# A twelve-stage perceiver: each layer norm is prepared in quarters inside the loop of the layer before

## The reference

```
def _layernorm(x, axis=-1, eps=1e-05):
    m = jnp.mean(x, axis=axis, keepdims=True)
    v = jnp.var(x, axis=axis, keepdims=True)
    return (x - m) / jnp.sqrt(v + eps)
...
x = x + _L0_xattn_ref(_layernorm(x), ctx_1024, ctx_1024, mask_BxSxS2_bk1, ...)
x = x + _L0_attn_ref(_layernorm(x), ...)
x = x + _L0_ffn_ref(_layernorm(x), ...)
...                       # L1: xattn, attn, ffn;  L2: xattn, attn, ffn;  L3: xattn, attn
x = x + _L3_ffn_ref(_layernorm(x), ...)
```

## Time and profile before

| | |
|---|---|
| median of 3 runs | 3710.66 us (3710.53 to 3714.74) |
| the profiled execution, its own time | 3704.09 us |
| its span, first to last instruction | 3702.4 us |
| mean granted TensorE clock | 0.913 of full speed |
| busy in the span | PE 3084.8 (83%), DVE 2010.6 (54%), ACT 1339.0 (36%), POOL 694.3 (19%) |

### The profile page before, as it was taken

The page is one execution under the profiler, slowest core; times in us unless marked ns, Lnnn a source line. Parts: engine busy times, 40 slices in busy tenths (PEclk is TensorE's granted clock), DMA queues, the critical chain, the costliest instruction groups (busy, mean ns, idle before and its releaser), DMA issues. The chain is left out here.

```text
span 3702.4 us, 64870 instructions
## 1 busy us (share of the span) xinstructions
PE 3084.8 (83%) x23914; PEld 1980.6 (53%) x23914; DVE 2010.6 (54%) x6137; ACT 1339.0 (36%) x3783; POOL 694.3 (19%) x1501
## 2 busy tenths in 40 slices
PE   6999987777779977887678885555999999999799
PEld 5888875555447755555446663333444444444465
DVE  4888875556236666669865556654232322332544
ACT  1444432333238762244367774432111111111222
POOL 1333330000027740033115652100000000000000
PEclk8999998988889998878689997777999999999899
DMA  3000000000011110210031100005000000000100
GB/s 90 25 24 25 26 21 1 1 1 1 4 34 43 42 36 3 56 43 1 16 62 38 34 25 15 1 1 176 1 1 1 1 1 1 1 1 1 39 1 12
DMA packets 164817, 83.61 MB, mean 23 GB/s; under 512 B 78803, under 2 KB 158678, under 8 KB 164310
## 3 DMA queue, kind: packets, MB, share of 16 engines
q1 hardware_dynamic: 164502, 79.47, 8.4%
HBM read 75.75 MB, written 3.67 MB: 21 GB/s over the span
## 5 line engine op out<-in xcount | busy, mean ns | idle before, releaser
L3074 PE MATMUL bank<-WhhT,hT 128*64 128x512 f32 (+1 forms) x4096 | 681.4, 488 | 29.6 <-ACT hT L3137 29.6
L3074 PEld LDWEIGHTS bank<-WhhT,hT 128*64 128x64 f32 x4096 | 285.7, 137 | 374.1 <-issue 256.4
L1188 POOL TENSOR_SCALAR probs<-probs,rinv 128x257 f32<-128x257 f32 x512 | 236.8, 482 | 169.8 <-DVE rinv L1099 169.7
L1005 ACT ACTIVATE probs<-probs,nbias 128x257 f32<-128x257 f32 x512 | 254.7, 507 | 0.0
L3226 DVE TENSOR_TENSOR pr<-hb,bank 128x512 f32<-128x512 f32 x32 | 22.0, 688 | 343.4 <-PE bank L3116 343.4
L3251 POOL COPY rb<-hT 128x512 f32<-128x512 f32 x32 | 35.7, 1117 | 919.8 <-ACT hT L3137 898.5
L925 PE MATMUL bank<-ident,probs 128*128 128x128 f32 x1024 | 141.0, 281 | 63.2 <-POOLq L1189 63.1
L729 POOL TENSOR_SCALAR probs<-probs,rinv 128x257 f32<-128x257 f32 x256 | 120.1, 482 | 277.0 <-DVE rinv L667 277.0
L925 PEld LDWEIGHTS bank<-ident,probs 128*128 128x128 f32 x1024 | 110.4, 141 | 93.6 <-POOLq L1189 84.9
L551 ACT ACTIVATE probs<-bank,nbias 128x257 f32<-128x257 f32 x256 | 119.3, 472 | 81.8 <-DVE rinv L667 71.1
L477 PE MATMUL bank<-kvT,qh 128*128 128x257 f32 x512 | 136.7, 391 | 4.5 <-ACT kvT L542 4.5
(11 more groups left out here) (658 smaller groups left out, 6874.9 us busy)
## 6 DMA issues: line engine op xcount, KB each, us to landing
kvT<-in_ctx_T SPq DMA_DIRECT2D x128, 128.5 KB
raw<-in_L_ffn_gru_w_hh SPq DMA_DIRECT2D x24, 512.0 KB, 4.7
kv<-in_ctx SPq DMA_DIRECT2D x64, 128.0 KB
kv<-in_ctx SPq DMA_DIRECT2D x32, 256.0 KB
W<-in_L_ffn_W SPq DMA_DIRECT2D x64, 64.0 KB, 2.2
v_last<-v_last SPq DMA_DIRECT2D x192, 8.0 KB, 1.7
mask_u<-in_mask_BxSxS_bk SPq DMA_DIRECT2D x64, 32.1 KB, 1.9
mask_u<-in_mask_Bx1xSxS_bf SPq DMA_DIRECT2D x64, 32.1 KB, 2.0
```

What stands on the lines that cost most here:

```text
L1005: i = e.activation(s, s, ACT.Exp, bias=self.nbias[v][:, r:r + 1], scale=self.scale, accum_out=self.rows_sum[v][:, r:r + 1])
L1188: e.tensor_scalar(s, s, self.rinv[v][:, r:r + 1], 1.0, ALU.mult, ALU.mult)
L3074: mm = e.matmul(self.bank[b][hf * BATCH:(hf + 1) * BATCH, 0:n], lhs, rhs, start=start, stop=stop, tile_position=(0, hf * BATCH))
```

## The change

X is loaded by four transfers, one for each quarter. Quarters 0, 1 and 2 of the next layer's norm are made in the loop of the layer before: VectorE takes the statistics once the last tile of the quarter has its update (`next_statistics`), and POOL makes the reciprocal root by Newton steps and the rows of y (`next_rows`). VectorE does all of quarter 3 after it has closed the stage. A tally `normed` takes the place of `norm_row`. ScalarE's Sqrt is removed from the norm; the stages that have a second norm of their own keep theirs. The last layer's norm runs over X in its normal order, and ScalarE puts yT in the order of time when it copies it; SP stores X behind the last quarter, and the reload is awaited only by the experts.

```diff
-    def norm_dve(self, e):
...
-    def norm_act_std(self, e):
...
+    def norm_statistics(self, e, layer, q):
+
+        tiles = range(4 * q, 4 * q + 4)
+        self.normed.wait_ge(e, 4 * (layer - 1) + q + 1)
+        for t in tiles:
+            e.bn_stats(self.stats[:, 6 * t:6 * t + 6], self.X[:, t * P:(t + 1) * P])
+        e.drain()
+        for t in tiles:
+            e.bn_aggr(self.moments[:, 2 * t:2 * t + 2], self.stats[:, 6 * t:6 * t + 6])
+        if q < 3:
+            e.drain().then_inc(self.measured.up(), 1)
+        else:
+            e.drain()
+            h, r, z = self.first_root(e, q)
+            for _ in range(3):
+                e.tensor_tensor(z, r, r, ALU.mult)
+                e.drain()
+                e.tensor_tensor(z, z, h, ALU.mult)
+                e.drain()
+                e.scalar_tensor_tensor(r, z, 1.5, r, ALU.add, ALU.mult)
+                e.drain()
+            self.norm_rows(e, q)
+            self.normed.wait_ge(e, 4 * layer + 3)
+            e.drain().then_inc(self.normed.up(), 1)
+
+    def norm_pool(self, e, layer, q):
+
+        self.measured.wait_ge(e, 3 * layer + q + 1)
+        h, r, z = self.first_root(e, q)
+        for _ in range(3):
+            e.tensor_tensor(z, r, r, ALU.mult)
+            e.drain()
+            e.tensor_tensor(z, z, h, ALU.mult)
+            e.drain()
+            e.tensor_scalar(z, z, 1.5, None, ALU.add)
+            e.drain()
+            e.tensor_tensor(r, r, z, ALU.mult)
+            e.drain()
+        self.norm_rows(e, q)
+        e.drain().then_inc(self.normed.up(), 1)
+
+    def first_root(self, e, q):
...
+        e.tensor_scalar(h, var, 1e-5, -0.5, ALU.add, ALU.mult)
+        e.drain()
+        e.tensor_scalar(r.bitcast(I32), h.bitcast(I32), -0.5, float(0x5f3759df - (1 << 30) - (1 << 22)), ALU.mult, ALU.add)
+        e.drain()
...
+    def norm_rows(self, e, q):
+        for t in range(4 * q, 4 * q + 4):
+            e.tensor_scalar(self.y[:, t * P:(t + 1) * P], self.X[:, t * P:(t + 1) * P], self.moments[:, 2 * t:2 * t + 1], self.rstd[:, t:t + 1],
+                            ALU.subtract, ALU.mult)
...
         for q in range(4):
+            p.normed.wait_ge(e, 4 * self.index + q + 1)
             for r in range(4):
                 t = 4 * q + r
-                self.n_row.wait_ge(e, t + 1)
                 i = e.transpose(p.bank[q][:, r * P:(r + 1) * P], p.y[:, t * P:(t + 1) * P], p.ident[:, :])
```

Where the calls stand, stage by stage (the same two calls in each):

```diff
 stage 0, VectorE
+            if u == 2 and t and t % 4 == 0:
+                self.x_added.wait_ge(e, t)
+                self.next_statistics(e, t // 4 - 1)
 stage 0, POOL, behind normalise(g + 2)
+            if u == 4 and t and t % 4 == 0:
+                self.next_rows(e, t // 4 - 1)
 stages 3 and 9, VectorE, at the end of a batch
+            if b == 1 and t > 4 and t % 4 == 1:
+                self.x_added.wait_ge(e, t - 1)
+                self.next_statistics(e, t // 4 - 1)
 stages 3 and 9, POOL, behind add_x
+            if b == 3 and t > 4 and t % 4 == 1:
+                self.next_rows(e, t // 4 - 1)
 stages 1, 2, 4, 5 and 10, VectorE, behind the update of a quarter (r < 3)
+                    e.drain()
+                        self.next_statistics(e, r)
 stages 1, 2, 4 and 5, POOL
+    def pool(self, e):
+        for q in range(3):
+            self.next_rows(e, q)
 stage 6, POOL, behind the addition of tile t
+            if t % 4 == 1 and t > 4:
+                self.next_rows(e, t // 4 - 1)
 stage 7, POOL, behind the addition of tile t
+                if t > 4 and t % 4 == 2:
+                    self.next_rows(e, t // 4 - 1)
 stage 8, POOL, behind the copy of Rb
+            if t > 4 and t % 4 == 3:
+                self.next_rows(e, t // 4 - 1)
 stage 11, SP and ScalarE
-        p.x_loaded.wait_ge(e, 1)
+        p.normed.wait_ge(e, 4 * (self.index + 1))
+            e.copy(by_time[:, 16 * q:16 * q + 16], p.bank[q][:, :].rearrange("p (b t) -> p b t", t=SEQ)).then_inc(self.n_yT.up(), 1)
 the program, VectorE's and POOL's queues
+            for q in range(4):
+                prog.x_loaded[q].wait_ge(e, 1)
+                prog.norm_statistics(e, 0, q)
             for s in stages:
                 closed.wait_ge(e, 4 * s.index)
                 s.dve(e)
                 e.drain().then_inc(closed.up(), 1)
+                s.x_final(e)
+                s.next_statistics(e, 3)
...
+            for q in range(3):
+                prog.norm_pool(e, 0, q)
 SP's queue
+            for q in range(4):
+                e.dma_start(four(prog.X)[:, 4 * q:4 * q + 4], x[:, 4 * q:4 * q + 4]).then_inc(prog.x_loaded[q].up(), 16)
```

More of the change, by code:

```diff
@@ L74, in __init__ @@
         self.rstd = self.fixed("rstd", [P, NT])
+        self.half, self.step = self.fixed("half_variance", [P, NT]), self.fixed("newton", [P, NT])
         self.stats = self.fixed("stats", [P, NT * 6])
@@ L1731, in dve @@
                 e.tensor_tensor(x, x, t1[:, :], ALU.add)
+                e.drain()
+                if g < 3:
+                    self.next_statistics(e, g)
             g = step - 2
@@ L1904, in dve, with pool @@
                 i.then_inc(self.x_done.up(), 1)
+                if x == E - 1 and r < 3:
+                    e.drain()
+                    self.next_statistics(e, r)
+    def pool(self, e):
+        for q in range(3):
+            self.next_rows(e, q)
 class L2CrossAttention(Stage):
@@ L2895, in dve @@
                 e.tensor_tensor(x, x, bank[2 + z][:, 0:P], ALU.add).then_inc(self.x_done.up(), 1)
+                if t % 4 == 3 and t < 12:
+                    e.drain()
+                    self.next_statistics(e, t // 4)
     def pool(self, e):
@@ L3549, in _ @@
         def _(e):
-            e.dma_start(four(prog.X), a["x"].rearrange("b t d -> (b t) d").rearrange("(t p) d -> p t d", p=P)).then_inc(prog.x_loaded.up(), 16)
+            x = a["x"].rearrange("b t d -> (b t) d").rearrange("(t p) d -> p t d", p=P)
+            for q in range(4):
+                e.dma_start(four(prog.X)[:, 4 * q:4 * q + 4], x[:, 4 * q:4 * q + 4]).then_inc(prog.x_loaded[q].up(), 16)
             stages[0].load_weights(e)
```

102 lines of the change are left out of this document (54 added, 48 removed).

## The result

| | before | changed |
|---|---|---|
| median | 3712.7 us (4 runs, 3710.5 to 3719.9) | 3840.3 us (4 runs, 3838.1 to 3842.3) |
| ratio, 95% interval | | 1.0345 (1.033 to 1.0361) |
| profiled execution: span, granted clock | 3702.4 us, 0.913 | 3840.6 us, 0.895 |
| busy: PE, DVE, ACT, POOL | 3084.8, 2010.6, 1339.0, 694.3 | 3130.8, 2002.7, 1323.6, 911.9 |

The kernel is 3.4% slower, about 128 us, where I had forecast 39. POOL works 218 us more. TensorE has the same instructions and is busy 46 us longer with them, so part of them ran at a lower clock. VectorE and ScalarE have less to do than before, and it did not help.

What follows compares the result with a forecast made beforehand. Twelve serial stages each have their own limit, mostly TensorE in the softmax attentions, with waits for the norm at starts. Starts +35.9, softmax loops -47.8, take-back +16, other loops -43.3 give 39.2 us slower: 3750 us, range 3685 to 3790.

Steps and rivals of the forecast that it cites:

- a late normalise handed on in a closed cycle: Stages 0, 3, 9: POOL's rows delay its next normalise, then turn, pT copy and reciprocal; in stage 3 by P - 0.8.
- P: POOL's time for one quarter's block, 14 small drained operations and 4 rows: 6.3 us.
- the third that the loops were to take back: Softmax loops of stages 0, 3, 9: TensorE's idle time absorbs a third of the 47.8 us loss, +16.
- the start of the program: Four X transfers instead of one put three more issues ahead of the weights: 0.9 us lost.
- The stage starts: Starts of stages 1-4, 6, 9-11: only quarter 3 remains after closing, some table loads go; 36.8 us gained.
- The two bounds: Limits on P from a small operation at 0.15 or 0.44 us: 3.8 and 7.8 us.
- Part 3: Loops other than the three softmax ones (stages 1, 4 to 8, 10): VectorE's statistics and POOL's late rows lose 43.3 us.
- the three loops: Softmax loops of stages 0, 3 and 9: POOL's blocks lose 15.6, 16.2 and 16.0 us, 47.8 before any take-back.
- Rival A: POOL's rows are hidden in its idle time, so the kernel gets faster: priced at 3685 us, chance 0.23.
- Rival C: POOL and VectorE lock each other at a shared port: 48 us more loss, 3798 us, chance 0.05.

Runs made afterwards that it cites:

- The first run: The changed kernel with all four quarters of layer 0's norm made by VectorE, none by POOL: 3824.4 us, 15.9 less than the changed kernel.

## Why the prediction was wrong

The direction was right, and so was the main mechanism, a late normalise handed on in a closed cycle. The size was off by a factor of three: 39 forecast, 128 measured, outside of my range. The steps that failed are the price P of a block, the third that the loops were to take back, the start of the program, where three blocks in series were left out, and TensorE's clock behind each wait, which the sum put at nothing. The terms, in the order of the sum:

- **The stage starts**, +36.8. Measured 32 (7.2, 5.8, 1.8, 4.6, 1.3, 3.9, 1.1 and, for stage 9, 6.4). The 1.3 that I booked for stage 1's second table load would lie in the table inside that stage and not in its start. Stage 3's start gained 4.1 at the matmul that I had named (L851), against 5.5, because it waits for the product L1084, which took 1.53 instead of 0.68 beside POOL's mask conversions, with the preparation ahead of it at 1.03 instead of 0.36. This matmul and its seven followers then took 5.90 instead of 3.65 at the low clock, which leaves 1.8. Stage 11's was 1.1, not 3.1.
- **The start of the program**, -0.9. This step failed by omission: it was 18.9 us. I had listed VectorE's part for layer 0 and the issues of X's transfers, but not POOL's three blocks in series, for which TensorE's transposes wait. With my own P = 6.3 they would have ended near 5 + 3 x 6.3 = 24 us, just about when the transposes were due; with 8.1 they ended at 30.1. So at my P the omission would have cost little; it is the long block and the low clock behind it that made it 18.9. The first run shows it: 17 of the 19 us went.
- **P**, 6.3. The small operations were priced right. The row of 0.37 was taken from multiplies, and the subtract doubles it: P = 8.1, above the bound of 7.8. The two bounds had varied the small operations alone and held the row at 0.37, so they left out the term that was wrong. For nine blocks this is 16 us. In the short stages it is 1.8 a block more as well.
- **"I take a third" back, +16.** Next to nothing was taken back. In stage 3 the difference stays constant to 0.01 us over the tiles that follow a step; in stage 0 at most 0.4 us and in stage 9 at most 0.7 come back behind one. The cycle from reciprocal over normalise, turn and copy to the next reciprocal is the limit, and TensorE's idle 16% is part of it. I had found the cycle myself and then allowed for the contrary.
- **The waits' second price**, not in the sum. In the wait of 7.3 us TensorE's clock fell to 1.2 GHz, and it was back only some 6 us after the turn had begun: 2.0 us a block, 18 us over nine, shown by the run with 52 transposes. In the kernel before, no wait in these loops is over 3.0 us once they run, but stage 1's start has one of 10.0, behind which 16 transposes take 4.51 us at a granted clock of 0.50: the information was there.
- **Part 3**, -43.3. Measured -69. Stage 4 with the start of 5 lost 11.4 where I had 3.5, stage 6 with 7 lost 13.3 against 10.5, stage 7 with 8 8.2 against 6, stage 8 16.9 against 13.3, stage 10 7.8 against 3, stage 5 1.8 against 2; stage 2's 0.8 was not in the sum. The places were right; that the 1.8 us of P go straight into the time where a block ends a stage is argued, not tested by itself. Stage 1's 9.0 against 5 is open, for the spread of that stage.

For the three loops: 47.8 - 16 = 32 forecast, 81 measured; 16 of the difference are P, 18 the clock, 16 the taking back. These three make up the whole of the 49. Of the three the clock was tested by itself and P was measured; the third is what is left.

Rival A, the hidden rows, needed P under 3.9 or idle time in long pieces. The run without Newton steps had 3.9 and was still 0.7% slower. But its idea was sound for pieces that are shorter than one gap: there most of the cost goes. Rival C, engines that lock each other, is out as the cause of the loops' loss: VectorE's instructions there kept their length, and POOL's rows cost the same in stage 2, with VectorE idle. It is not out elsewhere: beside the memset of the earlier trace rows, it shows at stage 3's start and in two of POOL's rows in stage 4, for 2 to 3 us of the 128.

## What to carry to other kernels

Work that is moved into a loop is to be cut to the length of the gap that it goes into, not compared with the engine's idle time in sum: 8 us at once cost 8.8, and the same 8 us in pieces of 0.7 to 1.7 cost between 0.1 and 1.5. If the loop is a closed cycle through that engine, as here, price a block at its full length less one gap and take next to nothing back (8.1 us cost 6.75 where TensorE's clock was held up), and look for a wait of that length elsewhere in the trace to see what TensorE's clock does behind it (here 2.0 us more). Look at what each moved helper does at the program's start too, where its calls lie in series with nothing to hide them.

## What the runs showed of the hardware

- On POOL a tensor_scalar of 128 by 128 in float32 took 0.37 us with a multiply or an add and a constant, 0.45 with multiply and add by two per-partition operands, 0.71 with a subtract and a constant and 0.79 with a subtract and two operands. On VectorE the same subtract and multiply took 0.34, and in a row they started 0.26 apart (on POOL 0.78). An operation on 4 columns took 0.20 to 0.23, and with a drain behind each they started 0.34 to 0.38 apart.
- A wait of 4.5 us on TensorE (the run with 24 transposes) brought its clock down as one of 7.3 did: in both the next turn took 1.97 us instead of 1.09. Behind a wait of 1.5 us it did not fall. Waiting is not the only thing that goes with the low clock: in the kernel before, from 36 to 52 us, TensorE is busy 15.6 of 16 us, and the granted clock is 0.50.
- Beside two POOL conversions of 128 by 1028 (1.07 and 1.05 us) a VectorE product of 128 by 512 with both operands in on-chip memory took 1.53 us instead of 0.68. Beside such products two POOL rows took 1.3 instead of 0.79. Beside POOL's rows VectorE's copies out of TensorE's banks kept their 0.69.
- One and the same stage of 1776 matmuls took between 374 and 393 us in the profiled executions of these kernels, with a mean granted clock of 0.92 in the fastest and 0.87 in the slowest. A comparison of a percent in such a kernel needs many runs.
